# Cross attention over 1500 keys: score halves and peak halves paired, in rounds of three key tiles

## What is computed

```python
q = split_heads(x_query @ Wq.T)      # 16 heads of 8
k = split_heads(x_kv @ Wk.T)         # x_kv: the 1500 context rows of this example
v = split_heads(x_kv @ Wv.T)
q, k = rope(q), rope(k)
attn = softmax(einsum('bhqd,bhkd->bhqk', q, k) / sqrt(8))
out = einsum('bhqk,bhkd->bhqd', attn, v)
x = x + out.reshape(B, T_q, 128) @ Wo.T
```

## Time and profile before

| | us |
|---|---|
| median of 3 runs | 1398.58 (1398.14 to 1403.32) |
| span of the profiled execution | 1397.8 |
| stretch of this stage's scores in it | 605.4 to 1294 |
| from one fold to the next, in the middle of the stage | 21.4 |

### The profile page before, as it was taken

One profiled execution on the slowest core, in us unless ns is written; L12 is line 12 of the kernel. 1 busy time (PEld: TensorE's weight loads), 2 busy tenths in 40 slices (PEclk: granted clock), 3 DMA queues, 4 the chain that ended last, 5 costly groups with the idle time before them and its releaser, 6 DMA issues.

```text
span 1397.8 us, 42378 instructions
## 1 busy us (share of the span) xinstructions
PE 1277.9 (91%) x17390; PEld 904.3 (65%) x17390; DVE 1066.3 (76%) x1817; ACT 802.5 (57%) x1760; POOL 842.5 (60%) x839
## 2 busy tenths in 40 slices
PE   6878999998997898678999999999999999988998
PEld 4556888788984666345565666656656666565986
DVE  6895676766677888777888888888888887886556
ACT  2542335336662333147677777777777777777541
POOL 6676232161567566578677786776777767665033
PEclk9887999999998999879999999999999999999999
DMA  5002700004521504546765465565565654546112
GB/s 139 2 1 68 244 3 2 2 28 131 163 59 29 78 12 89 104 133 134 156 136 145 118 129 134 113 139 130 112 145 133 114 139 96 120 85 186 43 49 54
DMA packets 84849, 136.19 MB, mean 97 GB/s; under 512 B 19809, under 2 KB 68322, under 8 KB 81314
## 3 DMA queue, kind: packets, MB, share of 16 engines
q1 hardware_dynamic: 80946, 125.87, 38.7%
q0 software_dynamic: 3712, 7.61, 1.9%
HBM read 98.38 MB, written 40.76 MB: 100 GB/s over the span
## 4 chain that ended last, share of the span: by engine, by line
PE 44%; ACT 6%; DVE 3%; issue 2%; POOL 2%; DMA 1%; ACTq 0%; POOLq 0%; SPq 0%; DVEq 0%
PE ps L2024 9%; PE ps L2040 8%; PE ps L1986 6%; PE ps L1977 6%; PE ps L2000 4%; ACT ARENA L2196 3%; ACT ARENA L2180 2%; PE ps L2502 2%; PE ps L2466 2%; DVE ARENA L2117 2%; PE ps L2513 1%; PE ps L2049 1%; PE ps L2476 1%; POOL ARENA L2245 1%; DMA key_parts<-ARENA 1%
## 5 line engine op out<-in xcount | busy, mean ns | idle before, releaser
L2117 DVE TENSOR_REDUCE ARENA<-ps 112x2 f32<-112x1000 f32 x384 | 456.3, 1197 | 109.7 <-PE ps L2000 108.0
L2196 ACT ACTIVATE ARENA<-ps 125x448 f32<-125x448 f32 x768 | 375.8, 546 | 106.5 <-PE ps L2024 103.7
L2245 POOL TENSOR_TENSOR ARENA<-ARENA 64x500 f32<-64x500 f32 x192 | 219.9, 1145 | 33.5 <-ACT ARENA L2174 9.1
L2024 PEld LDWEIGHTS ps<-ARENA 64*125 64x125 bf16 x3072 | 123.2, 134 | 143.3 <-ACT ARENA L2196 98.4
L2040 PE MATMUL ps<-ARENA 125*17 125x112 f32 x6144 | 210.3, 263 | 0.0
L2024 PE MATMUL ps<-ARENA 64*125 64x112 bf16 x3072 | 167.5, 228 | 28.7 <-ACT ARENA L2196 24.8
L2040 PEld LDWEIGHTS ps<-ARENA 125*17 125x17 f32 x6144 | 129.4, 97 | 57.3 <-issue 48.0
L2000 PE MATMUL ps<-ARENA 64*112 64x500 bf16 x768 | 153.7, 385 | 9.8 <-DVE ARENA L2117 8.9
L130 POOL TENSOR_TENSOR rs<-rs,mhalf 128x1 f32<-128x1 f32 x96 | 73.0, 762 | 122.4 <-DVE rs L125 122.1
L2251 POOL TENSOR_TENSOR ARENA<-ARENA 128x500 f32<-128x500 f32 x96 | 136.8, 1425 | 7.5
L2256 POOL TENSOR_TENSOR ARENA<-ARENA 128x500 bf16<-128x500 f32 x96 | 104.1, 1085 | 57.4 <-ACT ARENA L2180 57.4
(11 more groups left out here) (332 smaller groups left out, 2401.7 us busy)
## 6 DMA issues: line engine op xcount, KB each, us to landing
ARENA<-key_parts SPq DMA_DIRECT2D x192, 187.5 KB, 4.9
ARENA<-in_ctxT SPq DMA_DIRECT2D x96, 250.0 KB, 3.2
key_parts<-ARENA SPq DMA_DIRECT2D x64, 375.0 KB, 3.9
slots<-in_c_blank SPq DMA_DIRECT2D x2, 1472.0 KB, 12.8
results<-ARENA SPq DMA_DIRECT2D x42, 64.0 KB, 2.7
last_slots<-in_c_blank SPq DMA_DIRECT2D x1, 2144.0 KB, 12.5
ARENA<-in_L_ffn_W SPq DMA_DIRECT2D x1, 2048.0 KB, 8.5
ARENA<-in_L_ffn_W SPq DMA_DIRECT2D x4, 512.0 KB, 10.6
```

The costliest lines, as they stand in the source:

```text
L2024: m = e.matmul(ps[0:KT, b1[h], 112 * g:112 * g + 112], KS[b % 4][r, g, KT * kt:KT * kt + KT], Q1[r, b % 2, 112 * g:112 * g + 112], start=T ...
L2117: e.tensor_reduce(mxp[0:112, b % 2, 2 * g:2 * g + 2, ch], ps[0:112, b1:b1 + 2, 0:500], AX, ALU.max) \
L2196: e.activation(Pb[0:KT, n % NP_, 448 * h:448 * h + 448], ps[0:KT, b1[h], 0:448], ACT.Exp, bias=0.0, scale=1.0).then_inc(exped.sem, 1)
L2245: e.tensor_tensor(T2[r:r + 64, :], T0[64 - r:128 - r, n % 2, :], sin[64 - r:128 - r, sl], ALU.mult) \
```

## The change

A round is now three key tiles, that is six half scores. Each half score is paired with half a peak on the other half of the rows (`duo`): one score matmul, the peak matmul, three score matmuls. A tile's peak is spread over two duos, and DVE's maximum is a step of its own (`peaked`). A round on PE is

1. three duos,
2. the applies of the three tiles of the round before (48 matmuls in the trace's count, without a break),
3. three duos,
4. everything on the whole array: keys and values of this round, fold, turn, full, out, finish, one behind the other.

The other engines' steps stand in `mid` (between 2 and 3) or `end` (behind 4), `own` ahead of `mid`. A duo takes one bank of the ring of three, and so does each step of part 4. `Pb` has five buffers instead of four, and the arena grows by 600 words. The steps `blend` of one chunk are now three steps (`sine`, `cosine`, `total`), with the same instructions.

```diff
-            NP_ = 4
+            NP_ = 5
...
+                if b and b + 4 < B:
+                    for ch in range(3):
+                        full[1 + ch].insert(0, ("keys", b + 4, ch))
...
+                if b >= 1:
+                    full[0].append(("fold", b - 1))
+                    full[1].append(("turn", b - 1))
...
+                for n in range(0, B * NK, ROUND):
+                    b, kt = divmod(n, NK)
+                    mid, full, end = (x[kt // ROUND] for x in side(b))
+                    pb, p = (b + 1, 6 + kt) if kt < 6 else (b + 2, kt - 6)
+                    if pb < B:
+                        yield ("duo", b, kt, 0, pb, p, 1)
+                        yield ("duo", b, kt, 1, pb, p, 0)
+                        yield ("peaked", pb, p)
+                        yield ("duo", b, kt + 1, 0, pb, p + 1, 1)
...
+                    if n:
+                        for k in range(ROUND):
+                            yield ("apply", *divmod(n - ROUND + k, NK))
+                        if kt == 0:
+                            yield ("own", b - 1)
+                    yield from mid
+                    if pb < B:
+                        yield ("duo", b, kt + 1, 1, pb, p + 1, 0)
+                        yield ("peaked", pb, p + 1)
+                        yield ("duo", b, kt + 2, 0, pb, p + 2, 1)
+                        yield ("duo", b, kt + 2, 1, pb, p + 2, 0)
+                        yield ("peaked", pb, p + 2)
+                    yield from full
+                    yield from end
...
+                if step[0] == "duo":
+                    at[step] = banks[ring % len(banks)]
+                    ring += 1
...
+                elif kind == "duo":
...
+                    if free[b1]:
+                        w.wait_ge(*free[b1])
+                    free[b1] = exped(2 * n + h + 1)
...
+                    w.wait_ge(*free[bank])
+                    free[bank] = peaked(12 * pb + p + 1)
+                    for g in range(4):
+                        m = e.matmul(ps[0:KT, b1, 112 * g:112 * g + 112], KS[b % 4][own, g, KT * kt:KT * kt + KT],
+                                     Q1[own, b % 2, 112 * g:112 * g + 112], start=True, stop=True)
+                        if g == 3:
+                            m.then_inc(scored.sem, 1)
+                        if g == 0:
+                            m = e.matmul(ps[0:112, bank, 0:500], Q0[other, pb % 3, pg].rearrange("p j s -> p (j s)"),
+                                         KS[pb % 4][other, pg, 500 * ch:500 * ch + 500], start=True, stop=True)
+                            if ph == 0:
+                                m.then_inc(peak_mm.sem, 1)
```

More of the change, by code:

```diff
@@ L1687, in l1_xattn @@
             projected, joined = signal("projected", NT), signal("joined", NT)
+            ROUND = 3
+            FULL_ARRAY = ("keys", "values", "full", "fold", "turn", "out", "finish", "query", "route", "count", "turn_slots")
             def side(b):
[L1691 to L1699, removed]
@@ L1711, in side @@
[L1711 to L1716, removed]
+                mid, full, end = ([[] for _ in range(NK // ROUND)] for _ in range(3))
                 if b + 2 < B:
                     for q in range(3):
-                        f[2 * q].append(("values", b + 2, q))
+                        full[q].append(("values", b + 2, q))
@@ new lines, in side @@
+                if b == 1:
+                    full[0].append(("keys", 4, 2))
+                    mid[0] += [("stack", 3, 4), ("stack", 3, 5), ("sine", 4, 1), ("cosine", 4, 1), ("total", 4, 1)]
+                    end[0] += [("high", 4, 0), ("low", 4, 0)]
+                    mid[1] += [("sine", 4, 2), ("high", 4, 1), ("low", 4, 1), ("cosine", 4, 2), ("total", 4, 2)]
+                    mid[2] += [("high", 4, 2), ("low", 4, 2)]
+                    end[2] += [("write", 4, 0), ("write", 4, 1)]
+                    end[3] += [("stack", 4, i) for i in range(4)]
@@ L1745, in side @@
-                if b == 3:
[L1746 to L1760, removed]
@@ new lines, in side @@
+                return mid, full, end
+            parts = ("first", "earliest", "others", "second", "next", "picks")
+            last_steps = [(("cast", 0), B - 12, 3), (("route", 0), B - 6, 3), (("route", 1), B - 5, 11), (("exp", 0), B - 4, 0),
+                          (("choose", "chances"), B - 4, 1), *((("choose", part), B - 4, 2 + i) for i, part in enumerate(parts)),
+                          (("count", 0), B - 4, 8), (("pick", "bases"), B - 4, 8), (("pick", "places"), B - 4, 8)]
+            last_steps += [(("scatter", n, NK * (B - 4) + 10 + n), *divmod(NK * (B - 4) + 10 + n, NK)) for n in range(2 * LAST_SPLIT)]
@@ L1818, in early @@
+                    yield from full
+                    yield from end
+                yield ("begin", 0)
+                for k in range(ROUND):
+                    yield ("apply", B - 1, NK - ROUND + k)
+                yield ("own", B - 1)
             def early(t):
```

147 lines of the change are left out of this document (74 added, 73 removed).

## The result

| | before | changed |
|---|---|---|
| median of 4 runs, us | 1400.95 (1398.14 to 1406.4) | 1428.78 (1424.51 to 1430.7) |
| span of the profiled execution, us | 1397.8 | 1426.0 |
| fold to fold, mid-stage, us | 21.38 and 21.43 in turn | 21.97 and 22.27 in turn |

The ratio is 1.0173, with a 95% interval of 1.0142 to 1.0203: slower by 1.7%. The prediction was +18 us; the ratio says +24, the two medians and the two spans +28. Why the ratio is smaller than the quotient of the medians (1.020) the record doesn't say.

What follows compares the result with a forecast made beforehand. PE with its changes of shape was taken as the bound, ACT nearly reaching it. PE's work 18.67 plus waits 3.45 gave 22.1 us per example, 0.75 more; times 28, less 3, +18: 1417, range 1390 to 1440.

Steps and rivals of the forecast that it cites:

- waits for the ring at three places: PE held for banks of the ring of three, filled one by one: 3.45 us per example in all.
- the saved changes of shape: On PE, 16 changes of shape per example in place of some 32; PE's own work 1.87 us less, 18.67 against 20.54.
- Place 1: A round's first whole-array step waits for the fourth duo's bank, until its exponential ends: 0.35 x 4 = 1.4 us per example.
- Place 2: In an example's first round `own` and `high` stand ahead of the fourth exponential on ACT: 0.42 us more.
- the rival with the late chain: `high` ahead of a fourth exponential waits for POOL's rotated keys: 0.5 per example, 14 us more, 1431; chance 0.08.
- The rivals in which duos overlap badly: Score and peak halves don't run side by side well on PE: up to 0.45 a duo, 1431 to 1472; chance 0.12.
- the half rival: Short matmuls can't end before a longer one ahead: about 0.07 a duo, 16 us more, 1433; bad overlap's chance 0.12.
- The pairing itself gives nothing: On PE a duo takes 0.24 us, what its two halves take now, so pairing alone saves nothing.
- Place 3: A round's last whole-array steps hold banks that the next round's second and third duo need: mean 1.63 us per example.
- The stage's ends: Examples 28 and 29, lacking keys and then values, have short whole-array parts: 3 us less; the last 18 tiles unchanged.
- half the waits: Case within the denser-PE rival: at half the counted waits per example the time would be 1368; no chance of its own.
- the 1346: Rival: PE keeps its density, waits stay at 0.83, an example takes 19.5, 52 us less; under 1392 had chance 0.15.

Runs made afterwards that it cites:

- the halved copies: Changed kernel with ACT's copies of keys and values cut to about half their columns: 1469.65 us, ratio 1.013 to the kernel before on the same chip.
- the duo kernel: Kernel before, old order, each score and peak issued as two duos: 1391.51 us, ratio 0.9895; run again on the other chip 1426.33 us, ratio 0.9861.
- The kernel with the largest loss: Kernel before with duos, and the short steps moved from between the applies to ahead of keys or values: 1496.45 us, ratio 1.0368 to the kernel before.

## Why the prediction was right, and where it was not

**The forecast and its balance.** 22.1 per example was predicted, 22.12 is the mean of 21.97 and 22.27. Examples 0 to 27 were to lose 21 us and lost 21.2. The mechanism, waits for the ring at three places that outweigh the saved changes of shape, is what the trace shows. But that the numbers meet so closely is luck: two sizes in it are wrong in opposite directions (places 1 and 2 below), and so are the first four examples and the other 24, which were to lose 3 and 18 us and lost 5.6 and 15.6. The time as such, 1428.8, lies nearer to the 1431 of the rival with the late chain than to 1417; only the parts tell the two apart.

**PE's own work.** Three duos cost 0.85 and 48 applies 1.27, as worked out. The rivals in which duos overlap badly are out: at 0.45 a duo three would cost 1.48, and by the half rival's 0.07 a duo about 1.06. The Trainium skill's rule ("TensorE: Matmul & The Clock Gate", Part 3, what overlaps and what doesn't) that matmuls end in program order also across row groups does not show in the time: the next duo starts 0.21 to 0.27 behind a peak half whose modelled length is 0.37 to 0.41. The ends themselves are modelled, so the rule as such is neither shown nor refuted.

**"The pairing itself gives nothing"** was wrong, the one step of the mechanism that failed. I priced it by PE's work alone and compared the changed ring with the old one in one piece. The runs show no work more (two duos cost 0.58 in the old order, as score with peak did) and 0.7 us per example gained there (ratios 0.9895 and 0.9861), lost again when both banks are waited for (ratio 0.9992; fold to fold two thirds of it). In the rounds it is worth little: 22.12 with it, 22.30 without, and ratios of 1.0173 and 1.017. So the change is a loss by rounds of three, and the gain that half of it brings in the old order doesn't come with it.

**Place 1** (0.35 x 4) was oversized. The groups are 1.10, 1.11 and 1.19 instead of 1.2; less 0.85 that is 0.25, 0.26 and 0.34, about 1.1 for four. The exponential starts 0.50 behind its score, by ACT's timeline at 905.80, and PE goes on at 906.40, 0.05 behind the end of an exponential of 0.55, where the prediction took 0.14.

**Place 2** (0.42) was undersized. The first rounds have 0.44 more than the others in one example and 1.16 in the next, mean 0.8. The difference of 0.7 between the two is for the most part the 0.62 that `high` waits for POOL; the prediction had POOL's chain at nothing in its sum, and among the rivals at 0.5 an example. Places 1 and 2 together are 1.9 against 1.82 predicted, so two errors cancelled.

**Place 3** (1.63) holds: over the 0.85 of three duos the four rounds have about 1.6. Its account, that the copies are the holders, is half the truth, as the halved copies show: DVE's reads for fold and full stand right behind them.

**The stage's ends** were mis-sized. "In examples 28 and 29 ... I estimate 3 less" came out as 1.7 more, and example 30, which I left out, as 1.1 more. Examples 0 to 3 lost 1.4 each instead of 0.75. I have no experiment on either; the cause is open. The 4.4 us ahead of the first score are mostly in unchanged code, and I don't count them to the change: the same start is 614.9 in the duo kernel's profile.

One step of the rivals' arithmetic: half the waits gives 1371 us; 1368 comes out only with the 3 us of the stage's ends taken off as well, which the 1346 does not do.

Not found is an order in rounds of three that covers all three places. Whether more banks would do it wasn't tried: the peaks hold four, the applies one.

## What to carry to other kernels

Before steps are merged into longer groups, write the ring down bank by bank and compare, for each step, the time since its bank was filled with the time to empty it (here 1.1 to 1.2 us for a score, 1.8 to 1.9 for keys); the fewer and longer the groups, the less unrelated work stands between. Where a step fills several banks, wait for each bank at the matmul that needs it: that gave 1.0 to 1.4% here. And cover for one wait comes out of the cover of another, so a new order is to be costed at every reuse in the round, not at the one that it is meant to mend.

## What was not expected of the hardware

**POOL beside DVE.** The pair of POOL's tensor operations on the rotated keys takes 2.21 us as a rule, and 3.69 in the changed kernel at 909.67; a following one 2.28 instead of 1.24.

```profile
909.67 3.69 POOL L2284 TENSOR_TENSOR ARENA<-ARENA 64x500 f32<-64x500 f32 x2
...
914.47 2.28 POOL L2290 TENSOR_TENSOR ARENA<-ARENA 128x500 f32<-128x500 f32 x1
```

Beside each of the two long ones runs a DVE addition over two operands in SBUF:

```profile
910.63 0.67 DVE L2140 TENSOR_TENSOR ARENA<-ARENA 128x500 f32<-128x500 f32 x1
...
914.98 0.67 DVE L2140 TENSOR_TENSOR ARENA<-ARENA 128x500 f32<-128x500 f32 x1
```

Of the pair at 909.67 it is the first operation alone that is long, 2.55 instead of 1.07. From 700 to 1240 us the 105 operations of L2284 that have no DVE operation over two operands in SBUF beside them all take 1.06 to 1.07 and the 62 of L2290 all 1.24 to 1.26; the ten of L2290 that have one all take 2.27 or 2.28, and of the 39 of L2284 that have one most take 1.7 or more.

The Trainium skill ("SBUF — State Buffer", two separate sides) has the two engines share a port pair that the instruction that starts first holds to its end, a DVE operation with two SBUF inputs among them, while the other is blocked. That the two are in each other's way agrees with the trace. Who pays and how much doesn't: POOL's operation starts first (909.67 against 910.63, 914.47 against 914.98), the DVE addition keeps its 0.67, and POOL's gets 1.5 and 1.0 us longer. In the kernel before the addition falls elsewhere in POOL's chain, and there it is the one that gets longer in 23 cases (0.9 to 1.4 us). It was seen, not tested. The kernel with the largest loss has the same 3.69 in its chain (928.67 above), so this matters wherever ACT's `high` is close behind POOL.
